# A Trainium2 kernel of four normalised convolution layers: the first layer's branch projections regrouped by pixel piece

## The reference

```python
x = x + L0(_gn(x));  x = x + L1(_gn(x));  x = x + L2(_gn(x));  x = x + L3(_gn(x))

# L0, the layer that is changed: four branches m
y   = gelu(x[..., :, None] * w1)                  # w1: 32 channels x 4 branches
z   = gelu(einsum('bhwim,moi->bhwmo', y, wg))     # wg: one 32x32 matrix for each branch
out = einsum('bhwmc,cm->bhwc', z, w2)             # weighted sum over the four branches
```

## Time and profile before

| | us |
|---|---|
| median of 3 runs | 944.26 |
| the runs | 941.25, 944.26, 950.17 |
| profiled execution | 942.11 |
| its span in the trace | 940.3 |
| stage 1, first set: first Gelu to the end of the moments | 37.83 to 175.03 |
| stage 1, last set: the same | 379.42 to 558.43 |

### The profile page before, as it was taken

One profiled execution on the slowest core, in us unless ns is written; L12 is line 12 of the kernel. 1 busy time (PEld: TensorE's weight loads), 2 busy tenths in 40 slices (PEclk: granted clock), 3 DMA queues, 4 the chain that ended last, 5 costly groups with the idle time before them and its releaser, 6 DMA issues. The chain is left out here.

```text
span 940.3 us, 26232 instructions
## 1 busy us (share of the span) xinstructions
PE 747.4 (79%) x11376; PEld 523.0 (56%) x11376; DVE 597.5 (64%) x1081; ACT 502.8 (53%) x484; POOL 267.4 (28%) x305
## 2 busy tenths in 40 slices
PE   5588988499688798799998848968879979435664
PEld 5344444399566587566432228966557869112443
DVE  5556665799644378144686769984435756787771
ACT  4899999144355331777885533425543300444885
POOL 4511110463155200000000027404440000355993
PEclk9899999699799799799996778998998979855997
DMA  9423220000000000000000000000000000000778
GB/s 313 138 83 88 69 80 2 1 2 1 2 4 4 3 2 1 1 2 2 24 2 2 2 1 1 2 1 3 3 3 2 2 23 1 1 0 1 224 236 256
DMA packets 59921, 37.37 MB, mean 40 GB/s; under 512 B 1952, under 2 KB 59424, under 8 KB 59808
## 3 DMA queue, kind: packets, MB, share of 16 engines
q1 hardware_dynamic: 59808, 35.71, 12.6%
HBM read 18.93 MB, written 16.78 MB: 38 GB/s over the span
## 5 line engine op out<-in xcount | busy, mean ns | idle before, releaser
L772 ACT ACTIVATE work<-ps 128x2048 f32<-128x2048 f32 x64 | 120.0, 1875 | 56.1 <-PE ps L436 56.1
L454 PE MATMUL ps<-work,w2d 32*32 32x512 f32 x2048 | 141.7, 612 | 9.9 <-ACT work L772 8.5
L760 ACT ACTIVATE work<-X,l0s 128x2048 f32<-128x2048 f32 x64 | 133.4, 2087 | 16.9 <-POOLq L307 16.9
L436 PE MATMUL ps<-work,cst 32*32 32x512 f32 x2048 | 95.0, 643 | 22.2 <-ACT work L760 15.0
L1233 POOL TENSOR_TENSOR co<-mv,cst 128x1 f32<-128x1 f32 x7 | 1.3, 190 | 357.3 <-DVEq L307 297.7
L789 ACT ACTIVATE work<-ps 128x512 f32<-128x512 f32 x80 | 47.8, 597 | 98.7 <-PE ps L547 98.7
L454 PEld LDWEIGHTS ps<-work,w2d 32*32 32x32 f32 x2048 | 61.3, 105 | 64.7 <-issue 46.6
L558 PE MATMUL ps<-cst,work 128*128 128x143 f32 x640 | 93.9, 291 | 1.8 <-DVE X L1038 1.2
L558 PEld LDWEIGHTS ps<-cst,work 128*128 128x128 f32 x640 | 85.0, 194 | 2.6 <-ACT work L789 1.4
L952 DVE SCALAR_TENSOR_TENSOR X<-ps,X 128x1024 f32<-128x1024 f32 x32 | 39.1, 1223 | 56.5 <-PE ps L454 56.5
L547 PE MATMUL ps<-cst,work 128*128 128x128 f32 x320 | 50.7, 283 | 25.3 <-DVE work L1061 25.3
(11 more groups left out here) (130 smaller groups left out, 1340.7 us busy)
## 6 DMA issues: line engine op xcount, KB each, us to landing
out<-work SPq DMA_DIRECT2D x64, 256.0 KB, 3.2
work<-x SPq DMA_DIRECT2D x16, 512.0 KB, 5.2
work<-x SPq DMA_DIRECT2D x32, 256.0 KB, 3.2
work<-choose SPq DMA_DIRECT2D x8, 128.0 KB, 2.7
cst<-consts SPq DMA_DIRECT2D x1, 1009.5 KB, 9.2
cst<-consts SPq DMA_DIRECT2D x1, 64.0 KB, 2.0
```

What stands on the lines that cost most here:

```text
L436: last = pe.matmul(ps[C * k4:C * k4 + C, g, :], wg[rows, m, C * g:C * g + C], yb[rows, m % 2, k4 * BANK:(k4 + 1) * BANK], start=True, stop ...
L454: last = pe.matmul(ps[C * g:C * g + C, bank + b, :], diag[rows, m, :], zb[rows, k % ZDEEP, g, :], start=(m == 0), stop=(m == MULTI - 1))
L760: act.activation(yb[:, k % 2, :], X[:, s * PIX + i * CHUNK:s * PIX + (i + 1) * CHUNK], ACT.Gelu, scale=l0s[:, at:at + 1], bias=l0s[:, at + ...
L772: act.activation(zb[:, (s * UNITS + k) % ZDEEP, :, :], ps[:, 0:4, :], ACT.Gelu).then_inc(s_zs, 1)
```

## The change

- A unit is now a piece u of 512 columns with all four branches. `gelu_y` still works on 2048 columns of one branch, but `yb` holds all four branches of a chunk (4 x 4 banks), laid out alternately by branch and by piece so that a branch of the next chunk takes the place of the piece just projected. The fourth branch is split in two instructions of 512 and 1536 columns.
- `project_y(u)`: again 16 matmuls of 32 x 32 x 512, now with the branch as the column group, so the four branches come to lie on the partitions.
- `weigh_z(u)`: 4 matmuls of 128 rows x 32 columns x 512, one for each image, with one 128 x 32 matrix `w2d` that sums over the branches; bank 4 or 5 by turns; no accumulation over units.
- `add_piece(u)`: adds and measures 512 columns.
- TensorE's order is project(u + 1), weigh(u), background(u + 1). The background of the last set has 20 taps before the first projection, then 10 a unit up to unit 11, `sum_rows` in unit 12, `turn_rows` and the first `spread_pair` in unit 13, and one pair a unit in 14 to 28.
- The matrix w2d is made on VectorE after the barrier of stage 0 and no longer on GpSimd ahead of it; `zb` has three buffers instead of five.

```diff
-        yb, _e = part(0, [RING, CHUNK])
+        yb, _e = part(0, [4, 4, BANK])
...
-        TAPS_AT = {u: range(10 * u, min(10 * u + 10, W)) for u in range(13)}
...
+        TAPS_AT = {u: range(10 * u + 10 if u else 0, min(10 * u + 20, W)) for u in range(12)}
+        SUM_AT, TURN_AT = 12, 13
+        PAIR_AT = {TURN_AT + p: p for p in range(NB // 2)}
...
+                def project_y(u):
+
+                    i, j = divmod(u, 4)
+                    pe.wait_ge(s_y, (s * CHUNKS + i) * Y_OPS + (Y_OPS if j else MULTI))
+                    if s * UNITS + u:
+                        pe.wait_ge(s_zs, s * UNITS + u)
+                    for m in range(MULTI):
                         for g in range(G):
                             rows = slice(C * g, C * g + C)
-                            last = pe.matmul(ps[C * k4:C * k4 + C, g, :], wg[rows, m, C * g:C * g + C],
-                                             yb[rows, m % 2, k4 * BANK:(k4 + 1) * BANK], start=True, stop=True)
+                            last = pe.matmul(ps[C * m:C * m + C, g, :], wg[rows, m, C * g:C * g + C], y_piece(i, j, m)[rows, :],
+                                             start=True, stop=True)
...
+                def weigh_z(u):
+
+                    k = s * UNITS + u
                     pe.wait_ge(s_zs, k + 1)
...
+                    if k >= 2:
+                        pe.wait_ge(s_x1, k - 1)
                     for g in range(G):
...
+                        last = pe.matmul(ps[C * g:C * g + C, 4 + k % 2, :], w2d[:, :], zb[:, k % ZDEEP, g, :], start=True, stop=True)
+                    last.then_inc(s_acc, 1)
...
+                background(0)
+                project_y(0)
+                for u in range(UNITS):
+                    if u + 1 < UNITS:
+                        project_y(u + 1)
+                    weigh_z(u)
+                    background(u + 1)
                 stage_end(pe, s, 1)
...
+                def branch_y(i, m):
+                    if m < MULTI - 1:
+                        gelu_y(i, m, 0, 4)
+                    else:
+                        gelu_y(i, m, 0, 1)
+                        gelu_y(i, m, 1, 4)
...
+                for m in range(MULTI):
+                    branch_y(0, m)
+                for i in range(CHUNKS):
+                    for j in range(4):
+                        gelu_z(4 * i + j)
+                        if i + 1 < CHUNKS:
+
+                            branch_y(i + 1, j)
...
+            for m in range(MULTI):
+                rows = slice(C * m, C * m + C)
+                last = dve.tensor_scalar(w2d[rows, :], c("mean8", rows)[:, 0:C], c("w2", rows)[:, m:m + 1], float(B),
+                                         ALU.mult, ALU.mult)
+            last.then_inc(s_diag, 1)
...
+                def add_piece(u):
+                    k = s * UNITS + u
+                    piece = X[:, s * PIX + u * BANK:s * PIX + u * BANK + BANK]
+                    dve.wait_ge(s_acc, k + 1)
+                    dve.tensor_tensor(piece, piece, ps[:, 4 + k % 2, :], ALU.add).then_inc(s_x1, 1)
+                    dve.wait_ge(s_x1, k + 1)
+                    alone(dve)
+                    dve.bn_stats(stats[:, 6 * u:6 * u + 6], piece)
...
+                background(0)
+                for u in range(UNITS):
+                    add_piece(u)
+                    background(u + 1)
+                    if u == UNITS - 2:
                         if s + 1 == NS:
                             measure_first_v(NB - 1)
                         dve.drain()
...
             pool.wait_ge(s_const, 16)
-            for m in range(MULTI):
-                last = pool.tensor_scalar(diag[:, m, :], c("mean8")[:, 0:C], c("w2")[:, m:m + 1], float(B),
-                                          ALU.mult, ALU.mult)
-            last.then_inc(s_diag, 1)
```

More of the change, by code:

```diff
@@ L103, in build @@
         bns = sb("bns", 16)
-        w2d = sb("w2d", MULTI * C)
+        w2d = sb("w2d", C)
         head_of, place_of = sb("head_of", HEADS), sb("place_of", WS)
@@ L438, in project_y @@
                     last.then_inc(s_zp, 1)
-                def weigh_z(i, m, hf):
-                    n, k = s * (PIX // CHUNK) + i, s * UNITS + i * MULTI + m
+                def weigh_z(u):
+                    k = s * UNITS + u
                     pe.wait_ge(s_zs, k + 1)
[L444 to L450, removed]
-                    for g in range(G):
[L452 to L457, removed]
+                    if k == 0:
+                        pe.wait_ge(s_diag, 1)
+                    if k >= 2:
+                        pe.wait_ge(s_x1, k - 1)
+                    for g in range(G):
+                        last = pe.matmul(ps[C * g:C * g + C, 4 + k % 2, :], w2d[:, :], zb[:, k % ZDEEP, g, :], start=True, stop=True)
+                    last.then_inc(s_acc, 1)
@@ L480, in spread_pair, with background @@
                     last.then_inc(s_scb, 1)
-                def background(i, m):
-                    u = i * MULTI + m
+                def background(u):
                     if s + 1 < NS:
-                        for n in NEXT.get((i, m), ()):
+                        for n in NEXT.get(u, ()):
                             next_set(n)
@@ L489, in background @@
                             taps(0, w)
-                        if u == 13:
+                        if u == SUM_AT:
                             sum_rows(0)
-                        if u == 14:
+                        if u == TURN_AT:
                             turn_rows(0)
[L494 to L524, removed]
-                    background(i, 3)
-                    if not last_one:
-                        project_y(i + 1, 0)
-                    weigh_z(i, 3, 0)
-                weigh_z(PIX // CHUNK - 1, 3, 1)
+                        if u in PAIR_AT:
+                            spread_pair(PAIR_AT[u])
+                background(0)
[5 more added lines that the diff above has]
+                    background(u + 1)
                 stage_end(pe, s, 1)
@@ L995, in background @@
                                     measure_first_v(n - 1)
-                for i in range(PIX // CHUNK):
-                    for m in range(MULTI):
-                        background(i, m)
-                        if i and m == 0:
-                            add_half(i - 1, 1)
-                    if i == PIX // CHUNK - 1:
+                background(0)
[3 more added lines that the diff above has]
+                    if u == UNITS - 2:
                         if s + 1 == NS:
```

87 lines of the change are left out of this document (27 added, 60 removed).

## The result

The changed kernel takes 896.51 us (median of 4 runs, 895.62 to 900.62); the kernel before, run beside it, 942.80 (941.25 to 950.17). The ratio is 0.950, with a 95% interval of 0.944 to 0.956: 46 us faster, where 36 were predicted. The profiled execution took 900.62 us, with a span of 898.7 against 940.3.

What follows compares the result with a forecast made beforehand. ScalarE was taken to bound stage 1's first set, TensorE then VectorE its last; 0.35 + 3.1 + 32.6 = 36.1 us off 942.1 gave 906.0, with 2.15 for the median 908; likeliest 900 to 916, range 897 to 926.

Steps and rivals of the forecast that it cites:

- Weighting and the added mode: TensorE in stage 1: four tall tiles stream together as in line 454, 1.05 us; weighting starts 1.08 us after projection.
- Last set: Stage 1's last pass, from its first Gelu: TensorE bounds tap units, VectorE pair units; end at 146.4 against 179.0, 32.6 gained.
- First set: Stage 1's first pass, from its first Gelu: ScalarE bounds at 3.75 us a unit; 134.1 against 137.2, 3.1 us gained.
- First units at half clock: 1.4: Stage 1, first pass, units 0 to 3: projection and weighting twice as long at half clock, adding 1.4 us.
- The 0.35 us for the w2d instructions: Ahead of stage 1: GpSimd loses 1.38 us of work before its coefficients; gain between 0 and that, taken as 0.35.
- Stages 2 to 5 unchanged: The trace after would show no change in the stages behind stage 1; no gain was summed there.
- The median of the runs is 2.15 above that execution: Last step of the sum: 906.0 us for the profiled execution becomes a median of 908.
- 1: Rival on weighting in stage 1: tall tiles run one by one, 3.7 us instead of 1.05, giving 1019 us; chance 6%.
- 2: Rival on weighting in stage 1: column groups stream in two pairs, 1.9 us, giving 919 us; chance 9%.
- 5: Rival on pair units: TensorE still waits for VectorE at each pair, 5.3 us a unit, +18, 926 us; chance 6%.
- 3: Rival on pair units: TensorE's clock falls to half, 5.9 against 4.1 us, half the units, +13, 921 us; chance 13%.
- 4: Rival on VectorE's pair units: 3.75 us gives 903, 4.5 gives 914; counted inside the likeliest case, 66%.

## Why the prediction was off

The direction and the mechanism in stage 1 were right, and its two passes came within 2.4 and 0.2 us of the sum; the time lay half a microsecond under the range. Point by point:

- **Weighting and the added mode** were taken at 1.05 and 1.08 us; the trace has 1.07 and 1.08. The argument from line 454 held at full height.
- **Last set**, from its first Gelu: P(0) at 7.0 (7.3 said), P(12) 60.9 (60.2), P(13) 65.8 (65.1), P(14) 71.3 (70.7), P(29) 131.1 (131.2), P(31) 137.8 (137.9), the end at 146.2 (146.4). Tap units 4.50 (4.55, of which weighting holds TensorE for 1.02 and not 1.05), idle in unit 13 1.73 (1.8), pair units 4.07 (4.1), with VectorE shown to be their bound; the first four after z(15) still go at ScalarE's 3.74 to 4.02. That P(12) agrees so well hides two errors of opposite sign. P(2) came 6.06 us after P(1), where 4.55 was said, for the granted clock is 0.50 from 385.2 to 388.4 us; the prediction had full clock there. The shorter tap units and P(0) and P(1) made up for half of it.
- **First set** 131.7 us, 2.4 less than summed. Of the terms, "First units at half clock: 1.4" was 0.1: from z(0) to z(2) are 7.60 us, the full-clock 7.50, as the half-clock instructions still fit under ScalarE. "At a chunk boundary ... 7 x 0.1" did not appear: 26 units to z(28) (154.82) take 99.3, which is 26 x 3.75 and the 1.8 of the split. z(0) came 0.46 earlier. The last chunk (3 x 3.33 said, 10.1 measured) and the tail (6.0 both) were right. The 0.35 us for the w2d instructions did not show: the first coefficients of stage 1 start at 35.58 and 35.36 us before, and at 36.97, 35.37 and 35.57 after.
- **"Stages 2 to 5 unchanged"** failed. Stages 3 and 4 of the last set are 4.5 us shorter (134.5 in the mean of the four profiles of the kernel before and its two variants, 132.5 to 135.4; 130.0 in the ten of the regrouped kernel and its variants, 128.8 to 131.3), although their code is the same. My expectations for the repeated runs put all that down to scatter, which the table does not bear out for this stretch. The timelines of the same place, before and after:

```profile
651.88 0.56 PE L607 MATMUL ps<-work 64*64 64x65 f32 x20
654.12 0.63 PE L607 MATMUL ps<-work 64*64 64x65 f32 x12 [1.67 <-issue]
654.68 1.11 PE L591 MATMUL ps<-cst,work 128*128 128x128 f32 x4
```

```profile
613.69 0.33 PE L574 MATMUL ps<-work 64*64 64x65 f32 x5
614.33 0.68 PE L574 MATMUL ps<-work 64*64 64x65 f32 x27 [0.30 <-issue]
614.94 0.65 PE L558 MATMUL ps<-cst,work 128*128 128x128 f32 x4
```

  Before, TensorE stops for 1.67 us in the midst of one row of like instructions, waiting for nothing that the profile shows, and the next four of line 591 are 1.7 times as long; after, it stops for 0.30. All four profiles of the kernel before and its variants have three or four such pauses of 0.6 to 1.7 us there, and none of the ten others has one over 0.6. Summed they are 4.0, 3.6, 2.6 and 4.5 us, beside stretches of 135.2, 134.9, 132.5 and 135.4: over the 130.0 without any, the stretch is 5.2, 4.9, 2.5 and 5.4 us longer, so it goes with them, though not by their sum alone. What TensorE lacked is looked at in the last section.
- **"The median of the runs is 2.15 above that execution"** carried the sum over to the median. The profiled execution of after lay 4.1 us above its median instead. With -4.1 in place of +2.15 the forecast falls by 6.3 us. The 2.15 was scatter too: with the fourth run of the kernel before, its median is 942.80, 0.7 above the profiled execution. In the repeated runs of the changed kernel the median lies 0.0 and 2.4 above it.

The account by the spans: first set -5.5, last set -32.9, the last set's later stages -5.2, all else +2.0, together -41.6 us (940.3 to 898.7), where -36.1 was summed: 5.5 more, nearly all of it in code that the change does not touch. With the 6.3 of the offset that leads from 908 to 896.5. Either term alone would have left the time within the range; the two together passed its lower end, 11.5 us under the forecast. So two steps failed. The larger in this result is the last, "The median of the runs is 2.15 above that execution": it was -4.1. A single execution stood for a median, though runs from 941.25 to 950.17 lay in the table, and the range had no allowance for it. The one that comes again in every profile is "Stages 2 to 5 unchanged": put at nothing, it was 5.2 us in this pair and 4.5 in the means. By the two later medians (898.78, 899.82) the time lies within the range, so that it fell just outside is chance. That it is too low a gain is not: 908 is 8 to 12 us above all three medians.

Of the rivals, 1 was tested with its price built in and came out within 10 us of its time, and the 1.07 us of weighting rules out it and 2; a chain like that of 5 appears when the background is put first, and not in the changed kernel; 3 occurs, small; 4 is settled by the 4.07 us. Where the last set's gain comes from was argued as the pair units and their stalls. The starts of z bear that out for 24.6 us and add 9.9 ahead of z(15). The runs add that the gain needs the order and the short weighting together, and that the spread alone gives 0 to 6 us.

## What to carry to other kernels

When a queue holds both the work that the bounding engine waits for and background work that waits for a third engine, put the former first; here, in the regrouped kernel, that order alone decided between 0.95 and 1.06 of the time before. Spreading the background evenly pays only once no unit's background can block the next projection, and a step whose input was stored in the same unit belongs one unit later. Add the scatter between single executions and medians to a range, on both sides, before any mechanism is priced.

## What the runs showed of the hardware

Four fp32 matmuls of 128 rows x 32 columns, on four column groups with different data, stream together: 1.07 us for 8 instructions of 512 columns, and 0.87 us for eight more behind them, against 3.70 us for eight of 128 x 128.

TensorE paused for up to 1.67 us in the midst of like, ready instructions, only in the four profiles of the kernel before and its variants. They have 11376 matmul records; of the ten others, nine have 9840 and the one that weighs twice has 10352. The page's list of queues has the transfers of instructions (packets, MB, share), before, after, and weighing twice:

```profile
q8 instruction: 90, 1.47, 0.7%
```

```profile
q8 instruction: 78, 1.28, 0.6%
```

```profile
q8 instruction: 82, 1.34, 0.6%
```

1536 matmul records fewer go with 12 packets fewer, and 512 more with 4 more, 128 for each packet both times: this queue brings TensorE's instructions.

The Trainium skill (Runtime: NRT & Kernel Launch, "Instruction fetch mechanics") says that an engine's sequencer fetches its instructions in 16 KiB blocks by a DMA queue of its own, mostly hidden. The traces agree on the size: every transfer on q8 has 16384 bytes.

The traces also tie the pauses to these transfers. In these four profiles, all fourteen pauses over 0.6 us stand before one of the same four instructions, and these lie 378, 252 and 377 matmul records apart, which is 3, 2 and 3 times some 126. The shorter pauses of the ten others, 0.28 to 0.56 us, stand before four instructions too, 252, 377 and 252 apart. Each of the fourteen ends 2.15 to 2.90 us after a transfer on q8 starts, where 19 or 20 transfers lie in some 135 us. In the kernel before, one starts at 651.31 us and TensorE goes on at 654.12; in its variant with the first pair in unit 14, one starts at 645.29 and TensorE goes on, at the same instruction, at 647.45:

```profile
647.45 0.67 PE L607 MATMUL ps<-work 64*64 64x65 f32 x12 [1.66 <-issue]
```

So the 4.5 us are most likely waits for instructions. Why at most four of the 19 or 20 transfers of this stage are followed by such a pause in these kernels, and none in the regrouped ones, is not shown; no run moved the instructions and left everything else as it was.
